# The feature map of a linear attention: a Relu on ScalarE replaced by a maximum on VectorE

## The reference, cut to what matters

```
q, k, v = LN(x) @ Wq.T, LN(x) @ Wk.T, LN(x) @ Wv.T
q = q * cos + rotate_half(q) * sin          # the rotation; k the same
qf, kf = elu(q) + 1, elu(k) + 1             # the feature map
state += kf (outer) v;  z += kf             # along the 1024 positions
out = (qf @ state) / (qf . z + 1e-6)
x = x + LN(out @ Wo.T)
x = x + LN(keep_2_of_4(silu(LN(x) @ Wg) * (LN(x) @ Wu)) @ Wd)
```

## Time and profile before

| | |
|---|---|
| median of 3 runs | 1226.01 us (1225.1 to 1226.18) |
| span of the profiled execution, first to last instruction | 1224.5 us |
| the profiled execution's own time outside the profiler's span | not given; the median is 1.5 us above the span |
| TensorE busy | 1198.1 us, 98% |
| VectorE busy | 741.2 us, 61% |
| ScalarE busy | 550.4 us, 45% |
| GpSimd busy | 497.9 us, 41% |
| DMA | mean 74 GB/s |
| mean granted clock of TensorE | 0.996 |

### The profile page before, as it was taken

How to read it: one execution, slowest core, us unless ns; L and a number is a source line. 1 busy time by engine, 2 the same in 40 slices (tenths; PEclk the granted TensorE clock), 3 DMA queues, 4 the chain that set the end, 5 groups by cost and what they waited for, 6 DMA issues and landing times. The chain is left out here.

```text
span 1224.5 us, 16075 instructions
## 1 busy us (share of the span) xinstructions
PE 1198.1 (98%) x6014; PEld 1006.0 (82%) x6014; DVE 741.2 (61%) x1272; ACT 550.4 (45%) x1061; POOL 497.9 (41%) x403
## 2 busy tenths in 40 slices
PE   8899999999999999999998999999999999999997
PEld 7788888888888788888887878888888878888876
DVE  8656564645575556556564366677556655566568
ACT  5554555545545545455545433332323332333332
POOL 5433442514455425243235444342434653333415
PEclk9999999999999999999999999999999999999999
DMA  7231322222334223222133322121113321111211
GB/s 232 74 86 37 85 69 52 78 52 70 89 92 121 69 61 87 65 76 68 35 80 111 112 60 82 38 70 35 53 52 104 112 78 43 53 52 43 60 44 69
DMA packets 50349, 90.31 MB, mean 74 GB/s; under 512 B 6496, under 2 KB 6752, under 8 KB 50272
## 3 DMA queue, kind: packets, MB, share of 16 engines
q1 hardware_dynamic: 50272, 89.29, 25.8%
HBM read 64.09 MB, written 8.39 MB: 59 GB/s over the span
## 5 line engine op out<-in xcount | busy, mean ns | idle before, releaser
L1244 POOL TENSOR_TENSOR w_lo<-stage,w_hi 128x512 fp32r<-128x512 f32 x96 | 129.6, 1364 | 258.9 <-ACT w_hi L802 258.1
L510 PE MATMUL bank_q<-x_hi,w_hi 128*128 128x512 f32 x436 | 175.2, 402 | 1.3 <-DVE scratch L1025 1.3
L512 PE MATMUL bank_q<-x_lo,w_hi 128*128 128x512 f32 x436 | 171.3, 393 | 0.0
L511 PE MATMUL bank_q<-x_hi,w_lo 128*128 128x512 f32 x436 | 170.7, 392 | 0.0
L1244 POOL TENSOR_TENSOR big_lo<-hidden,big_hi 128x512 fp32r<-128x512 f32 x30 | 69.0, 2319 | 192.8 <-ACT big_hi L922 192.8
L913 ACT ACTIVATE scratch<-hidden 128x512 f32<-128x512 f32 x64 | 40.6, 634 | 206.9 <-DVE hidden L1165 206.9
L1244 POOL TENSOR_TENSOR big_lo<-q_rows,big_hi 128x1024 fp32r<-128x1024 f32 x31 | 76.3, 2460 | 77.4 <-ACT big_hi L844 77.2
L1062 DVE TENSOR_SCALAR small<-bank_od 128x4 f32<-128x4 f32 x61 | 9.7, 159 | 153.5 <-PE bank_od L636 97.5
L511 PE MATMUL bank_y<-wout_hi,a_lo 128*128 128x512 f32 x256 | 100.6, 393 | 0.0
L512 PE MATMUL bank_y<-wout_lo,a_hi 128*128 128x512 f32 x256 | 100.6, 393 | 0.0
L510 PE MATMUL bank_y<-wout_hi,a_hi 128*128 128x512 f32 x256 | 100.5, 393 | 0.0
(11 more groups left out here) (333 smaller groups left out, 3022.4 us busy)
## 6 DMA issues: line engine op xcount, KB each, us to landing
q_rows<-scratch SPq DMA_DIRECT2D x124, 128.0 KB, 2.3
x_rows<-x SPq DMA_DIRECT2D x48, 256.0 KB, 3.0
stage<-wq SPq DMA_DIRECT2D x32, 256.0 KB, 2.8
stage<-wo SPq DMA_DIRECT2D x32, 256.0 KB, 2.7
stage<-wg SPq DMA_DIRECT2D x32, 256.0 KB, 2.7
stage<-wu SPq DMA_DIRECT2D x32, 256.0 KB, 2.8
stage<-wd SPq DMA_DIRECT2D x32, 256.0 KB, 2.7
x<-x_rows SPq DMA_DIRECT2D x16, 256.0 KB, 2.6
```

Of the source, the lines that this page charges most:

```text
L510: pe.matmul(ps, whi, xhi, start=first, stop=False, skip_group_check=True)
L511: pe.matmul(ps, wlo, xhi, start=False, stop=False, skip_group_check=True)
L512: return pe.matmul(ps, whi, xlo, start=False, stop=last, skip_group_check=True)
L1244: return pool.tensor_tensor(dst, full, hi.bitcast(F32), ALU.subtract)
```

## The change

The rotation's sum adds 1, so that what is stored and transferred is y = x + 1. Exp gets a bias of -1, and so still gives exp(x); the bias is a column of the tile `small`, set once by a memset. The last step takes max(min(exp(x), 1), y) where it took min(exp(x), 1) + relu(x). The two are equal up to rounding: for negative x exp(x) is at least x + 1, for positive x the minimum is 1 and y is larger. The Relu instructions of ScalarE (L827 and L838) go, and Exp raises the semaphores that they raised. On VectorE the sums L1030 and L1048 become instructions with three operands (two tensors and a constant) and two additions; the steps L1035 and L1052 stay of that form, with the second operation changed.

```diff
-        mhalf, sign = small[:, 0:1], small[:, 3:4]
+        mhalf, minus, sign = small[:, 0:1], small[:, 1:2], small[:, 3:4]
...
             def key_terms(p):
                 g.wait_ge(dve_kx, p + 1)
-                act.activation(Ek, xk, ACT.Exp)
-                act.activation(xk, xk, ACT.Relu).then_inc(act_ke, 1)
+                act.activation(Ek, xk, ACT.Exp, bias=minus).then_inc(act_ke, 1)
...
             def query_terms(j):
                 _, _, grown, whole = pair_of(j)
                 pair_landed(g, j)
-                act.activation(grown, whole, ACT.Exp)
-                act.activation(whole, whole, ACT.Relu).then_inc(act_qe, 1)
+                act.activation(grown, whole, ACT.Exp, bias=minus).then_inc(act_qe, 1)
...
             def rotate_sum(j):
-                dve.tensor_tensor(part, part, turned, ALU.add).then_inc(dve_x, 1)
+                dve.scalar_tensor_tensor(part, part, 1.0, turned, ALU.add, ALU.add).then_inc(dve_x, 1)
...
             def query_sum(j):
-                dve.scalar_tensor_tensor(whole, grown, 1.0, whole, ALU.min, ALU.add).then_inc(dve_f, 1)
+                dve.scalar_tensor_tensor(whole, grown, 1.0, whole, ALU.min, ALU.max).then_inc(dve_f, 1)
...
             def rotate_keys(p):
-                dve.tensor_tensor(xk, xk, rotk, ALU.add).then_inc(dve_kx, 1)
+                dve.scalar_tensor_tensor(xk, xk, 1.0, rotk, ALU.add, ALU.add).then_inc(dve_kx, 1)
...
             def key_sum(p):
-                dve.scalar_tensor_tensor(xk, Ek, 1.0, xk, ALU.min, ALU.add).then_inc(dve_kf, 1)
+                dve.scalar_tensor_tensor(xk, Ek, 1.0, xk, ALU.min, ALU.max).then_inc(dve_kf, 1)
...
+            dve.memset(minus, -1.0)
```

## The result

The changed kernel takes 1219.05 us (median; 1218.53 to 1220.20) where the kernel before, run beside it, takes 1225.55 (1224.43 to 1226.18): 6.5 us less, ratio 0.9950, 95% interval 0.9936 to 0.9964. A second pair of runs, one of the experiments, gave 1220.03 against 1226.09, ratio 0.9952 (0.9936 to 0.9967). The forecast was 1221.4, that is 4.6 us less, with a range of 1218.3 to 1224.2. Direction and place were right. The sum was 1.5 us short in this pair of traces (6.1 against 4.6) and 0.7 short in the second pair (5.3); the ratio's interval (4.4 to 7.8 us) is too wide to part forecast and result, so the difference is worked out from the traces only.

The account below looks back on a forecast made before the run. TensorE, busy 98% of the span, was taken as the bound, with gains only where it waits for ScalarE. 3.4 + 1.2 = 4.6 us off 1226.0 gave 1221.4 us, range 1218.3 to 1224.2.

Parts of the forecast that it names:

- Bound: Whole kernel: TensorE, busy 98%, bounds it; the change wins only where TensorE stands still and ScalarE is the reason.
- (a): Four longer TensorE stalls at L608 (53.07, 154.89, 401.33, 648.08 us) each shorten by 0.85 us: 3.4 us.
- sign of being wrong: Idle ahead of L608 near 52.2 us should fall to 0.3; wrong if the first of four stalls keeps its length.
- (b): Shorter TensorE stalls (567.43, 484.15, about 70.7 and 323.9 us) vanish: 0.42, 0.29 and twice 0.25, together 1.2 us.
- (c): At 653.22 us TensorE's 2.03 us idle, waiting for GpSimd's residual, moves along with TensorE: no gain, no loss.
- (d): At 144.31, about 390.7, 474.7 and 557.9 us scalings wait for VectorE's reciprocal, without Relu in the chain: nothing counted.
- (e): The opening: VectorE and GpSimd take turns, L1035 still starts near 36.9 us, so it gives 0, plus or minus 0.1.
- rival 3: The opening: L1035 gets its turn ahead of GpSimd, TensorE's idle there goes, 3.9 us more gained, 1217.5 us; 6%.
- Rival 1: At 654 us the clock stays up, saving 1.6 of about 1.8 us lost in matmuls: 1219.8 us; 20%.
- Rival 2: Behind 648.08 and 401.33 us TensorE's wait for GpSimd takes back 0.85 us each: 1223.1, with a third 1224.0; 14%.
- Rival 4: On VectorE the sum with two additions runs at half speed, L1030 taking 2.43 instead of 1.22: 1232 us; 4%.
- rival 5: ScalarE isn't shortened, because Exp with a column costs as much more as Relu did; 1%.

Follow-up runs that it names:

- both kernels again: No edit: the kernel before and the changed kernel each run once more, 1225.88 us (1.0000) and 1220.03 us (0.9952).
- the change in the opening only: Changed kernel with Relu left out only for query pairs 0 and 1 and the first keys, kept for all later ones: 1227.10 us, 1.0012.
- queries only: Changed kernel with the keys' Relu, plain Exp and old sums put back: 1219.62 us, 0.9950.
- the column alone: Kernel before with a column of zeros as the bias of its Exps, Relu and plain sums kept: 1227.93 us, 1.0013.
- the other order: Query pair's Exp moved behind the next slot's four scalings on ScalarE: 1214.85 us in the changed kernel, 1215.66 in the kernel before with its Relu.
- the reordered, changed kernel: Changed kernel with the query pair's Exp moved behind the next slot's four scalings on ScalarE: 1214.85 us, 0.9911.
- the memset alone: Kernel before with one more small memset on VectorE at the start, of a column nobody reads: 1226.24 us, 0.9996.

## Why the prediction was right, and where it was short

The shift of each L608's start, after less before, gives what each step brought: -1.47 us at the first, -2.62 at 154.89, -4.23 at 401.33, -5.14 at 567.43, -6.14 at 648.08, and it stays at about that to the end.

In the second pair of traces (both kernels again) the same shifts are -1.30, -2.61, -3.39, -4.40 and -5.41 us.

*Bound.* Right but for one place. TensorE stands still less and does the same work; time went where ScalarE ended its wait, and at 323.93, where GpSimd did, fed by ScalarE's copies behind the Relu.

*(a)* 3.4 us forecast. Measured 0.85, 0.77, 1.17 and 0.91: 3.7 us. The first is 1.47 less the opening's 0.62. The 1.17 at 401 is above a Relu's length; in the second pair the four are 0.83, 0.90, 0.34 and 0.92, 3.0 us, so the place at 401 moves by 0.8 from pair to pair, and the mean of the two sums, 3.35, is what was forecast. The forecast of the remaining idle times was right at 152.27 (0.51 for 0.45) and 641.94 (0.77 for 0.8), within 0.3 at 397.10 (0.62 for 0.9), and wrong at 51.60 (1.88 for 0.3), because it left out that TensorE arrives earlier at a wait whose end is set by a transfer: 0.6 us by the earlier scores, and the rest because the clock no longer fell on the way (0.83 over 40 to 50 us before). The prediction named as a sign of being wrong that this first stall keeps its length. It even grew, and still the time was won there: from the first query projection to this L608 the changed kernel takes 0.93 us less than the one with the change in the opening only, which still has the Relu ahead of it. The sign was badly chosen, not the term.

*(b)* 1.2 us forecast: 0.33, 0.31, 0.29 and 0.44, 1.37 us (second pair 1.5). The 0.31, at 323.93, is not "of the kind of 484.15": it was a wait for GpSimd's residual, which the saving brought forward, so the size was right there and the mechanism was not. These are four stalls, where the prediction's last part speaks of five.

*(c)* 0 forecast, and 2.03 us of idle stays 2.03.

*(d)* 0 forecast: 0.05, 0.11, 0.05 and 0.09, together 0.3 us. Small, but the second pair gives the same 0.3 us.

*(e)* Forecast 0, plus or minus 0.1; it gave about 0.3 in this pair, and 0.3 more that are the execution's start. In the changed kernel the mechanism is as forecast: without Relu the query sum comes while GpSimd holds its turn, and takes 2.94 us. But it took the landing of the query's transfer as given, and that moved from 33.31 to 36.22 us between traces of kernels without these Relus; with the landing at 36.22 GpSimd's turn is over and sets nothing. Mis-sized was the end of GpSimd's turn, 36.9 where it was 36.35. The prediction carried L1048's collision over from the earlier trace rows, which then pushes the keys' Exp to 32.88; in the changed kernel the collision isn't there, the keys' sum ran at 31.92, in front of GpSimd's second residual, and didn't push it back. The Trainium skill's rule of an exclusive lock (SBUF — State Buffer, section "SBUF: two separate sides") is borne out: 0.91, 1.42, 1.74 and 2.94 us for instructions of 0.69 and 1.22 that meet a residual of GpSimd. So the two engines also wait for each other without a semaphore. (By durations alone (e) would have been rival 3, not the last rival, as the prediction has it.)

*The sum.* 0.62 + 3.7 + 1.37 + 0.3 is 6.0 us, some 0.15 more lie in steps of under 0.1; the span says 6.1. Against 4.6: 0.3 from the start, 0.3 from the opening, 0.3 from (a), mostly at 401, 0.2 from (b), 0.3 from (d), 0.15 from the rest. None decides by itself. In the second pair 0.7 us of the 1.5 are not there: 401 gave 0.8 less, and the start 0.06 instead of 0.3, while other places gave some 0.3 more. So about half of the shortfall is what two executions differ by, and the rest lies in terms of 0.1 to 0.4 us.

*Instructions.* The column's 0.10 us measured 0.09; the VectorE forms nothing. 

*Rivals.* Rival 1, the clock staying up at 654 us, was not so: 0.97 over 640 to 700 us in both executions of the changed kernel. Yet it can be: with queries only the clock held 1.00 there, and its price, 1.6 us, was right. From the L510 that ends the long wait to the next L608 it is 5.11 us in the kernel before (653.22 to 658.33, the clock at 0.57 over 654 to 658 us) and 3.49 with queries only:
```profile
648.11 0.47 PE L510 MATMUL bank_s<-big_hi,k_hi 128*128 128x512 f32 x1 [2.02 <-issue]
...
651.60 0.60 PE L608 MATMUL bank_s<-ident,scratch 128*128 128x128 f32 x4
```
From the same L510 to the end of the span it is 571.3 us in both profiled executions of the kernel before and in the changed kernel (571.4 in its second), and 569.7 with queries only. That kernel reached the place 1.0 us later than the changed one, so its whole time, 1219.62 us, doesn't show it. With the column alone the clock fell too (0.97), but ahead of the L510, which starts 5.14 us behind its L608 all the same; there 569.7 us follow, and the fall cost nothing. Rival 2 (given back at the next wait) did not occur behind 401 or 648: the L510 behind each moved with its L608. Rival 3 had 0.3 us of an opening, and not its 3.9. Rival 4 falls with the 1215 ns of L1028, rival 5 with the 1153 of the Exp. 

What the prediction didn't ask is why Relu was on the path. The two runs with the other order show it: not by its length but by its place in ScalarE's queue, behind an instruction that waits for a transfer and in front of the scalings on which TensorE waits. Moving the pair was worth 10.9 us of 1226.6 and left 0.8 us for the change, give or take some 2 us.

## What to carry to other kernels

Work taken from an engine that is 45% busy pays only where that engine ended the bound engine's wait, by itself or through an engine that it feeds: 43 us of Relu gave 6, and those for the keys gave none. Before shortening such an instruction, ask what stands behind it in its queue; if that doesn't depend on it, reorder first, and measure the shortening then. Count the gain by start times against the other trace, not by idle times: an engine that arrives earlier at a transfer's landing shows more idle time and has lost nothing.

## Of the hardware, not expected

- A constant bias given as a number leaves Exp at 1062 ns for 128x1024; as a 128x1 column it takes 1153.
- One added memset of one column, at 1.3 us, goes with a shift of VectorE's place against GpSimd 30 us later: the second key sum (L1048 before) took 0.69 us in all eleven traces of kernels that have it, and 1.75 or 1.76 in the three without, with no change in the kernel's time from the memset alone. The cause is open.
- The granted clock's falls move between kernels of the same work: over 640 to 700 us it was 0.97 in both kernels, and 1.00 with queries only and with the reordered, changed kernel; over 40 to 70 us 0.94 before and 1.00 after. A fall behind the long wait near 650 us cost 1.6 us; one ahead of it, or ahead of the first L608, cost nothing, because the wait's end is set by another engine or a transfer.
